# TensorE's order within a unit of attention: turns, projections and values' product, then the score

## The reference

```python
x = x + xattn(layernorm(x), ctx, ctx, mask)        # Q = ln(x) wq, K = ctx wk, V = ctx wv, rope on Q and K
#   scores = Q K^T / sqrt(32), masked; attn = softmax(scores); out = (attn V) wo
x = x + ffn(layernorm(x))                          # router, top 2 of 8 experts, shared part
```

## Time and profile before

| what | value |
|---|---|
| time, median of three | 1389.66 us |
| profiled execution | 1386.94 us, span 1385.1 us |
| TensorE matmul busy | 1331.2 us (96%) |
| TensorE weight load busy | 1025.7 us (74%) |
| VectorE busy | 961.9 us (69%), some 90% while attention lasts |
| ScalarE busy | 817.9 us (59%) |
| GpSimd busy | 584.2 us (42%) |
| granted TensorE clock, mean | 0.993 |

### The profile page before, as it was taken

The page is one execution under the profiler, slowest core; times in us unless marked ns, Lnnn a source line. Parts: engine busy times, 40 slices in busy tenths (PEclk is TensorE's granted clock), DMA queues, the critical chain, the costliest instruction groups (busy, mean ns, idle before and its releaser), DMA issues.

```text
span 1385.1 us, 28144 instructions
## 1 busy us (share of the span) xinstructions
PE 1331.2 (96%) x8063; PEld 1025.7 (74%) x8063; DVE 961.9 (69%) x2631; ACT 817.9 (59%) x1919; POOL 584.2 (42%) x724
## 2 busy tenths in 40 slices
PE   7998999999999999999998999999999999999996
PEld 6666676766767777677666777777778888888885
DVE  6898889889898898988887666666653434333432
ACT  2889789888898887988983222222213333333342
POOL 4443524435244343443263532222344555555543
PEclk9899999999999999999999999999999999999999
DMA  6555465564654646455565322222258769885552
GB/s 218 160 147 144 139 192 151 161 180 135 194 146 146 186 137 195 145 145 159 156 203 181 92 85 92 92 84 93 71 174 208 218 134 283 193 197 107 104 81 34
DMA packets 145636, 206.47 MB, mean 149 GB/s; under 512 B 35279, under 2 KB 72655, under 8 KB 145490
## 3 DMA queue, kind: packets, MB, share of 16 engines
q1 hardware_dynamic: 124274, 167.04, 39.2%
q0 software_dynamic: 17952, 33.64, 12.9%
q10 hardware_dynamic: 3264, 4.00, 0.9%
HBM read 105.35 MB, written 69.35 MB: 126 GB/s over the span
## 4 chain that ended last, share of the span: by engine, by line
PE 67%; DVE 12%; issue 7%; DMA 4%; SPq 4%; POOL 3%; ACT 2%; DVEq 0%; POOLq 0%; ACTq 0%
PE psum L1502 13%; PE psum L1504 13%; PE psum L1503 13%; PE psum L782 6%; PE psum L694 6%; DVE a_probs L955 4%; PE psum L803 4%; SPq L384 3%; PE psum L731 2%; PE psum L732 2%; PE psum L733 2%; PE psum L1569 1%; PE psum L1598 1%; DMA w_halves<-a_w_lo 1%; DVE a_probsT L961 1%
## 5 line engine op out<-in xcount | busy, mean ns | idle before, releaser
L955 DVE CUSTOM_DVE_ANT_0 a_probs<-psum,a_bias 128x512 f32<-128x512 f32 x512 | 341.9, 685 | 56.6 <-PE psum L782 52.8
L597 ACT ACTIVATE a_probs<-a_probs,a_low 128x512 f32<-128x512 f32 x512 | 368.8, 724 | 9.5 <-DVE a_low L955 9.5
L694 PEld LDWEIGHTS psum<-a_ident_r,a_probs_bits 128*128 128x128 f32 x2048 | 224.5, 141 | 69.9 <-ACT a_probs L597 20.5
L782 PE MATMUL psum<-a_kT,a_q_stack 128*128 128x512 f32 x512 | 244.1, 478 | 25.3 <-DVE a_low L955 19.0
L694 PE MATMUL psum<-a_ident_r,a_probs_bits 128*128 128x128 f32 x2048 | 245.5, 243 | 3.9 <-ACT a_probsT L603 1.4
L603 ACT ACTIVATE a_probsT<-psum 128x512 f32<-128x512 f32 x328 | 195.6, 597 | 55.8 <-PE psum L694 54.6
L1371 POOL DMA_INDIRECT out<-b_y,b_pairs_sb x71 | 112.6, 1586 | 147.3 <-DMA out<-b_y,b_pairs_sb 84.2
L961 DVE COPY a_probsT<-psum 128x512 f32<-128x512 f32 x184 | 126.0, 685 | 4.1 <-PE psum L694 3.0
L782 PEld LDWEIGHTS psum<-a_kT,a_q_stack 128*128 128x128 f32 x512 | 96.3, 188 | 40.5 <-DVE a_low L955 21.7
L1805 DVE SCALAR_TENSOR_TENSOR b_v_hidden<-b_v_hidden,psum 128x256 f32<-128x256 f32 x71 | 29.9, 421 | 134.4 <-ACT b_v_hidden L1467 134.4
L523 POOL CAST a_w_hi<-a_w_raw 128x256 fp32r<-128x256 f32 x96 | 38.3, 399 | 197.3 <-DMA w_halves<-a_w_lo 122.9
(11 more groups left out here) (219 smaller groups left out, 2956.4 us busy)
## 6 DMA issues: line engine op xcount, KB each, us to landing
b_w<-w_halves SPq DMA_DIRECT2D x16, 1536.0 KB, 11.1
a_q_stack<-a_qT_hi SPq DMA_DIRECT2D x254, 64.0 KB, 2.0
a_q_stack<-a_qT_lo SPq DMA_DIRECT2D x253, 64.0 KB, 2.0
w_halves<-a_w_hi SPq DMA_DIRECT2D x96, 128.0 KB, 2.0
w_halves<-a_w_lo SPq DMA_DIRECT2D x96, 128.0 KB, 1.9
a_xT_in<-in_x_turned SPq DMA_DIRECT2D x32, 256.0 KB, 2.9
a_ctx_in<-in_ctx SPq DMA_DIRECT2D x32, 256.0 KB, 3.0
a_x_in<-in_x SPq DMA_DIRECT2D x32, 256.0 KB, 3.5
```

Source lines behind the costliest of these rows:

```text
L597: nc.scalar.activation(probs[:, h % 2, t], probs[:, h % 2, t], ACT.Exp, bias=low[:, h % H, t:t + 1], scale=-1.0, accum_out=total[:, h // G ...
L694: last = nc.tensor.transpose(out[:, P * i:P * (i + 1)].bitcast(F32R), src(i), ident_r[:])
L782: nc.tensor.matmul(psum[:, t % 2], q_stack[:, stack_slot(h), P * t:P * (t + 1)], kT[:, batch, at // REP], start=True, stop=True).then_inc( ...
L955: nc.vector.tensor_tensor_reduce(probs[:, h % 2, t], psum[:, t % 2], bias[:, t], 1.0, HUGE, ALU.add, ALU.min, low[:, h % H, t:t + 1]).then ...
```

## The change

In TensorE's loop over the units, the score of unit u + 6 moves from before `beside` to behind it:

```diff
             for u in range(H * TT):
                 turn_probs(part, b, u // TT, u % TT)
+                beside(part, b, par, u)
                 if u + AHEAD < H * TT or part != "last":
                     scores(b, par, (u + AHEAD) // TT, u % TT ^ 2)
-                beside(part, b, par, u)
```

## The result

The changed kernel takes 1418.37 us (median of 3 runs, 1415.46 to 1420.65) against 1389.66: a ratio of 1.0178, 95% interval 1.0143 to 1.0213, which is 24.7 us of 1389.66 (20 to 30); the medians stand 28.7 apart. Run again beside the kernel before on another chip it took 1415.63 against 1394.50: 1.0157 [1.0134, 1.0179], or 21.9 us (19 to 25). The ratios are those of the record and not the quotients of the medians shown: these would be 1.0207 and 1.0152, and in the experiments they lie up to 0.2% from the ratio. One execution each of the kernel before, of e3_products and of g2_only1 took 3099 to 6050 us; these count in the medians but not in the ratios. The forecast, 14.4 us more by its sum and 1404 in all, had the sign and, of the two ratios, 58% and 66% of the size. The profiled execution took 1415.46 us, its span 1413.6, and the granted clock has a mean of 0.991.

A forecast was written before the change was run, and what follows sets the result against it. VectorE was taken to bound each batch to about step 35, TensorE from step 36. Six middle batches at 2.1 (12.6), first 0.3 and last 1.5 sum to 14.4 us, forecast 1404 us, range 1390 to 1413.

The forecast's parts named there:

- step 1: Values' product early in a batch: score comes at the product's end, minimum 1.23 us later, VectorE 0.9 late after cover.
- The adds: TensorE waits for VectorE's "add" at step 43, step 57 and the batch's end: 0.85, 0.65 and 0.65 us.
- Step 29, given back: Chunks fill the score's wait: TensorE 0.5 us ahead, VectorE 0.2 late, its idle gap swallowing the product's loss.
- The products of steps 17, 33 and 49: The other values' products of a batch, where VectorE has more backlog or an idle gap behind: put at 0.
- Step 35: Keys' turn waits for GpSimd: the 0.5 us lead is lost, +0.3; taken as +0.2 a batch, bounds -0.5 and +0.5.
- First and last batch: First batch has no "add": 0.3 us. Last has three, with more room between: 1.5 us.
- The copies, L970: VectorE's copy of the inverse sums, four times a batch: an unknown, taken as 0 with 4 us either way.
- The statements on what would show it: Signs in the changed profile: late score at step 1, "add" releasing with 0.5 to 0.7 us, period up about 2.
- Filled waits: Rival: work fills TensorE's waits for minima, each of seven batches gains about 1 us, 1382 us; chance 0.12.
- no change: Rival: VectorE reaches each "add" with room, only some tenths of a us a batch remain, 1389 to 1392; chance 0.11.
- VectorE bounds throughout: Rival: product losses are not given back at step 29, 3.5 us a batch, +24, 1414 us; chance 0.13.

The follow-up runs named there:

- e3_products: Kernel before with the score behind the step's work only in the values' product steps 1, 17, 33 and 49: 1404.50 us, 1.0056 times the kernel before.
- g2_only1: Kernel before with the score behind the step's work in step 1 alone: 1396.52 us, 1.0027 times the kernel before.
- e6_add: Changed kernel with VectorE doing "add" before the minimum in every step that has one: 1411.65 us, 1.0132 times the kernel before.
- e2_back: Kernel before with the score behind the step's work only in steps 35 to 63: 1407.52 us, 1.0086 times the kernel before.
- g3_adds: Kernel before with the score behind the step's work only in steps 41, 55 and 62, before or at the adds: 1402.04 us, 1.0050 times the kernel before.
- e1_front: Kernel before with the score behind the step's work only in steps 0 to 34: 1402.99 us, 1.0058 times the kernel before.
- f2_q12: Changed kernel with the two chunks that wait for rotated queries moved from step 29 to 30: 1418.45 us, 1.0181 times the kernel before.
- f1_step1: Changed kernel with the score first, as before, in step 1 only: 1409.86 us, 1.0111 times the kernel before.
- e8_before_kt: Kernel before, old order everywhere, with the second turn of keys and its copy two steps later: 1389.66 us against 1394.29, 0.9969.
- e0_after: The changed kernel run again, unaltered, on another chip: 1415.63 us against 1394.50 for the kernel before, 1.0157.
- e5_kt: Changed kernel with the second turn of keys and its copy two steps later: 1413.45 us, 1.0139 times the kernel before.
- g1_undo: Changed kernel with the score first in step 1, "add" before the minimum and the keys' turn two steps later: 1397.83 us, 1.0022 times the kernel before.

## Why the prediction was right or wrong

**Direction and kind of cost: right.** Nothing is added, and nearly all of the cost is waiting: in the attention windows TensorE's matmul row is busy only 2.1 of the 27.0 us longer, and the first half-clock stretch, worth 1.0, lies in that phase. At step 1 the score stands at the product's end, as forecast. Timeline of TensorE, changed kernel, steps 0 to 2:

```profile
307.22 0.46 PE L782 MATMUL psum<-a_kT,a_q_stack 128*128 128x512 f32 x1
307.52 0.46 PE L694 MATMUL psum<-a_ident_r,a_probs_bits 128*128 128x128 f32 x4
307.91 3.64 PE L803 MATMUL psum<-a_probsT,a_v 128*32 128x512 f32 x32
311.48 0.50 PE L782 MATMUL psum<-a_kT,a_q_stack 128*128 128x512 f32 x1
```

And VectorE's minimum of that score:

```profile
312.17 0.69 DVE L955 CUSTOM_DVE_ANT_0 a_probs<-psum,a_bias 128x512 f32<-128x512 f32 x1 [1.74 <-PE psum L782]
```

From the turn to this minimum it is 4.65 us, where the earlier trace rows give 3.29: 1.36 later, 1.23 was said. Before, VectorE did not wait here.

**The adds: right in place, near in size.** Step 43, changed kernel, TensorE and then VectorE, to be laid beside the earlier trace rows:

```profile
369.80 0.47 PE L782 MATMUL psum<-a_kT,a_q_stack 128*128 128x512 f32 x1 [0.18 <-DVE a_low L955]
370.11 0.46 PE L694 MATMUL psum<-a_ident_r,a_probs_bits 128*128 128x128 f32 x4
370.92 0.50 PE L731 MATMUL psum<-a_wo_hi,a_attT_hi 128*128 128x512 f32 x1 [0.35 <-DVE a_x_res L989]
...
371.72 0.39 PE L782 MATMUL psum<-a_kT,a_q_stack 128*128 128x512 f32 x1
371.95 0.46 PE L694 MATMUL psum<-a_ident_r,a_probs_bits 128*128 128x128 f32 x4
```

```profile
370.18 0.69 DVE L989 TENSOR_TENSOR a_x_res<-psum,a_x_res 128x512 f32<-128x512 f32 x1
```

"Add" starts at 370.18, the chunk that it releases at 370.92, 0.74 behind, and score and turn follow. The same at step 57 and the batch's end, where it releases the next batch's turn:

```profile
391.05 0.50 PE L731 MATMUL psum<-a_wo_hi,a_attT_hi 128*128 128x512 f32 x1 [0.65 <-DVE a_x_res L989]
...
399.21 0.53 PE L694 MATMUL psum<-a_ident_r,a_probs_bits 128*128 128x128 f32 x4 [0.60 <-DVE a_x_res L989]
```

Shifts of the means: +0.51 at step 43 (0.85 forecast); +0.85 at 57, of which 0.15 comes back (0.65); +0.69 at the end (0.65). That is 1.90 against 2.15. The step before the first of them, 42, adds 0.38 that the forecast did not have: its score waits for a minimum (the 0.18 above), and e6_add leaves it as it is. That the back half costs 12.0 us by e2_back, and three late steps alone 7.0 by g3_adds, bears out the place. e6_add takes only 3.5 us off; the shift that its batches bring to step 36 is 0.46 larger than the changed kernel's, so a part was lost again ahead of the adds.

**The step that failed: "Step 29, given back".** I let TensorE be 0.5 us ahead there and the product's loss be swallowed by an idle gap of VectorE. Measured: turns come 1.04 us late at step 6, 0.3 to 0.9 between steps 7 and 25, 1.03 at step 30 and 1.09 at step 34. Over the batches it is 0.08 to 1.87 at step 34, never a lead. The front half, for which the sum had 1.5 us, costs 8.1 (5.6 to 10.5) by e1_front. Timeline of TensorE at step 29, changed kernel:

```profile
347.39 0.46 PE L694 MATMUL psum<-a_ident_r,a_probs_bits 128*128 128x128 f32 x4
348.54 0.47 PE L731 MATMUL psum<-a_wq_hi,a_xT_hi 128*128 128x512 f32 x1 [0.69 <-DVE a_q_sin L915]
...
350.00 0.39 PE L782 MATMUL psum<-a_kT,a_q_stack 128*128 128x512 f32 x1
```

On VectorE, the instruction that frees that bank and the minimum of step 27, which frees the score's:

```profile
347.53 0.86 DVE L915 SCALAR_TENSOR_TENSOR a_q_sin<-psum,a_rstd,a_rope_q 128x256 f32<-128x256 f32 x2
348.31 0.68 DVE L955 CUSTOM_DVE_ANT_0 a_probs<-psum,a_bias 128x512 f32<-128x512 f32 x1
```

And TensorE's turn of step 29 in the kernel before:

```profile
335.53 0.50 PE L694 MATMUL psum<-a_ident_r,a_probs_bits 128*128 128x128 f32 x4
```

Two things in that step were wrong. First, where the two engines stand. The sum left TensorE's turn of step 29 where it was and VectorE 0.9 late. In this batch, counted from the turn of step 1, the turn of step 29 comes 39.87 us later and not 38.62, so TensorE is itself 1.25 late before the step's first wait; the minimum of step 27 comes 40.79 later and not 39.00, so VectorE is 1.79 late. Second, the filling. I had put chunks into the score's wait as if chunks waited for nothing, but the first one's bank is freed by VectorE, too (0.69 us), and the score now queues behind it: 2.61 us lie between turn and score, where the lengths of a turn and two chunks make 0.29 + 2 x 0.69 = 1.67. The second is not enough by itself, for f2_q12, which takes these chunks out of step 29, is 2.08 late at step 31. Within the working there is a slip as well: a VectorE 0.9 late reaches the minimum of step 29 at 338.36 and not at 338.22, which makes it 0.33 late in place of 0.2.

How much of this loss is step 1's own is less sure. f1_step1, which undoes step 1 alone, takes the shift at step 34 from +1.09 to -0.29. g2_only1, late in step 1 alone, puts +1.07 on the turns from 6 to 18 and +0.8 at step 34, but that is hardly more than e8_before_kt shows there with the old order (+0.78), and its 3.8 us are half a us a batch. So the product makes turns 1.07 late by step 6, its price is 3.8 us (1.1 to 6.4) alone and 6.4, not clear of noise, within the changed kernel. What is left of the front half's 8.1 is then its other late scores', which no run took singly. The products of steps 17, 33 and 49, which the sum had at 0, may be a part of it: all four cost 7.8 us (4.9 to 10.7) by e3_products, 4.0 more than step 1 alone, though the two intervals overlap.

**Step 35: no lead was there to lose.** The term was +0.2 behind it (a lead of 0.5 lost, and a little more), and what is measured there is +1.47. Of that 1.09 is brought from step 34, which is the failed step above, and 0.38 is added in steps 34 and 35 (0.37 in e0_after). Changed kernel, TensorE, beside the earlier trace rows:

```profile
358.69 0.46 PE L694 MATMUL psum<-a_ident_r,a_probs_bits 128*128 128x128 f32 x4
361.06 0.36 PE L716 MATMUL psum<-a_ident_r,a_k_stack 128*128 128x128 f32 x2 [1.90 <-POOL a_k_stack L494]
361.25 0.47 PE L782 MATMUL psum<-a_kT,a_q_stack 128*128 128x512 f32 x1
361.56 0.46 PE L694 MATMUL psum<-a_ident_r,a_probs_bits 128*128 128x128 f32 x4
```

GpSimd's timeline tells what comes before the keys:

```profile
356.89 0.40 POOL L523 CAST a_w_hi<-a_w_raw 128x256 fp32r<-128x256 f32 x1 [2.23 <-DMA w_halves<-a_w_lo]
357.37 0.73 POOL L525 TENSOR_TENSOR a_w_lo<-a_w_raw,a_w_hi 128x256 fp32r<-128x256 f32 x1
358.06 1.31 POOL L498 TENSOR_TENSOR a_q<-a_q,a_q_sin 128x512 f32<-128x512 f32 x1
...
360.71 0.29 POOL L494 CAST a_k_stack<-a_k_stack 128x128 fp32r<-128x128 f32 x1 [0.17 <-POOL a_k_stack L491]
```

GpSimd works in its order: it had stood 2.23 us for a transfer, then does weights, the queries' sum and the keys. The prediction had it follow VectorE. In this batch it followed a transfer as well: the first of these instructions starts 49.37 us after the turn of step 1, and 47.50 in the kernel before; what made the transfer later was not traced. So in f1_step1, where TensorE is early, the keys' wait swallows the lead (2.40 us in that batch). Moving the keys takes 4.3 us from the kernel before (e8_before_kt) and 2.5 from the changed one (e5_kt), and the two intervals overlap, so whether the changed order gains less from it is open.

**First and last batch.** The first was put at 0.3 and grew by 2.6. By its turns it loses 1.1 at step 35, where the keys' turn waited 1.24 for an evacuation of VectorE (L961), and 1.0 at step 49, which is the half-clock stretch shown with the result: there TensorE's instructions took longer. The wait of 1.27 us ahead of it, for values (L934), was there before with 0.96. The last was put at 1.5 and grew by 1.5, and that is luck: I had three adds in mind, but TensorE's matmuls wait for "add" once there, 1.2 us in both kernels. Its turns come 2.4 us late by one wait of 2.13 for a transfer of the queries' stack (at 726.02), and some of that is made good behind it.

**The copies, L970.** 0 with 4 us either way was said. The source view of the changed kernel, against the earlier trace rows:

```profile
L970 DVE COPY a_inverse_wide<-a_inverse x32: 426/556/1467, 59.0 to 750.6; 128x512 f32<-128x512 f32 x32
```

The longest are alike, but the median went from 428 to 556 ns and the sum from 20.2 to 25.6 us: 5.3 more VectorE time. What stretches a copy can be read off the two timelines. Changed kernel, fourth batch, GpSimd and VectorE:

```profile
328.75 1.29 POOL L503 TENSOR_TENSOR a_attT_lo<-a_att,a_attT_hi 128x512 fp32r<-128x512 f32 x1
328.86 1.47 DVE L970 COPY a_inverse_wide<-a_inverse 128x512 f32<-128x512 f32 x1
```

The copy starts while GpSimd's instruction runs, and ends at 330.33, some 0.28 behind that one's end. So it is every time in this trace: of the 32 copies 19 start inside an instruction of GpSimd and end 0.28 to 0.29 us behind its end (481 to 1467 ns), the other 13 start beside none and take 426 to 428 ns. In the kernel before 12 are stretched (441 to 1433 ns), with the same 0.28. Five others start inside an instruction of GpSimd and are not: two where it ended within the copy's first 0.1 us, and three at the small L472. An instruction of GpSimd that started only after the copy never stretched it; it was then itself late: in ten of eleven such cases of the kernel before, L503 ended 1.15 us behind the copy. So the reordering put 7 more copies behind a start of GpSimd's. How much of the 5.3 us reached the end no run separates.

**The statements on what would show it.** Score and minimum of step 1 and "add" as a releaser came out, the latter with 0.60 and 0.65 us as said at two places and 0.35 at step 43, where 0.5 was the least. Feed-forward came out but for 1.0 us, beside its half-clock stretch. "The period grows by about 2" was too small (3.87, or near 3 with the reserve on the trace of before). "Waits of TensorE for minima shrink" missed: they grew by 2 to 4 us. That VectorE's for scores don't shrink was right, but they grew by 40, which nothing in the sum had.

**The rivals.** Filled waits and no change are out: no kernel with the new order was faster. "VectorE bounds throughout" gave 1414, nearest to the time, and its premise, the loss not given back at step 29, was the right one; its other 0.5 us a batch, for a second product, no run took singly. Its mechanism was not: VectorE, idle for 92.9 us before minima instead of 52.8, bounds less than before. So its near hit is luck in part. The Trainium skill (Perfetto Trace Analysis, Identifying the Most-Contended Engine) would take the engine of highest occupancy, VectorE with 44.52 of 50.12 us in the first stretch. The trace disagrees in this sense: both engines got idler as the time grew, because each waits for the other in order.

**What stays open.** Of the 21.9 us, undoing three places takes 18.8 (g1_undo against e0_after), of which the keys' move is not the change's own; for the rest no single suspect is shown. The single undoings gave 6.4, 3.5 and 2.5, which sum to 12.4, 6 less than the three together. The intervals of these runs are 3 to 6 us to each side, so that difference may be noise. A lead gained at one place and lost at the next would make one, but no run took them in pairs: it is not shown.

## What to carry to other kernels

When two engines wait for each other in order, a gap seen in the trace of before is not cover to be counted on. Ask first whether the engine would still arrive there as early as before (here it came 1.25 us late), and then what releases each instruction that is to lie in the gap (here the first chunk waited 0.69 for the same late engine). What the other engine waits for belongs first in the step, and a step's filler behind it; where three of 64 steps broke this, it cost 7 us. And an instruction that waits for a third engine's queue (here the keys' turn at step 35) can swallow a lead gained before it, so move it first: it gave 0.3% in the kernel before, with nothing else changed.

## What was not expected of the hardware

A copy of one form, 128x512 f32 on VectorE, took 428 ns at the median before and 556 after, up to 1467, with nothing in it changed. All 31 stretched ones in the two traces had started while an instruction of GpSimd ran, and ended 0.28 to 0.29 us behind its end.

TensorE's clock was at its lower level for 3.4 us twice in the changed kernel's trace, each time soon after TensorE had stood still (1.27 and 1.86 us), and not at all between 44.4 and 1379.0 us in that of before. A reordering that only adds waiting may so also cost clock, here some 1 us a time.

The medians of the kernel before differed between comparisons by 4.8 us (1389.66 and 1394.50), more than the 2.8 us that I had taken for the bound of what can be told: for edits of that size only comparisons on one chip count.
